# Reordered routed loop, a narrower block table, set 2's low parts on VectorE and no GpSimd drain at the end, in a gated-channel plus mixture-of-experts kernel

## The reference, cut to what matters

```python
def reference(x, cfc_w, bn_w, bn_b, router_w, w1, v1, w2, shared_gate, shared_up, shared_down):
    x = x + conv_gate(_ln_c(x))        # per channel gate from mean, max, std over pixels and a median
    t = _to_tokens(x)                  # 2048 tokens x 512 channels
    h = _ln_t(t)
    logits = h @ router_w.T            # 8 experts
    top_vals, top_idx = top_k(logits, 1)
    out = zeros_like(h)
    for e in range(8):                 # each token only counts for its expert
        out += dense_w[:, e:e+1] * ((silu(h @ w1[e]) * (h @ v1[e])) @ w2[e])
    out += (silu(h @ shared_gate.T) * (h @ shared_up.T)) @ shared_down.T
    return _from_tokens(t + out)
```

## Time and profile before

| what | value |
|---|---|
| median of 3 runs | 459.75 us (457.16 to 459.96) |
| the profiled execution's own time | 459.99 us |
| its span (first to last instruction) | 458.3 us |
| TensorE busy | 384.1 us, 84% of the span |
| VectorE, ScalarE, GpSimd busy | 264.0, 159.9 and 171.1 us |
| mean granted TensorE clock | 0.943 over the span, 1.00 from 250 to 440 us |
| TensorE busy from 300 to 350 us | 50.0 of 50 us |

### The profile page before, as it was taken

The page is one execution under the profiler, slowest core; times in us unless marked ns, Lnnn a source line. Parts: engine busy times, 40 slices in busy tenths (PEclk is TensorE's granted clock), DMA queues, the critical chain, the costliest instruction groups (busy, mean ns, idle before and its releaser), DMA issues.

```text
span 458.3 us, 7143 instructions
## 1 busy us (share of the span) xinstructions
PE 384.1 (84%) x1870; PEld 312.7 (68%) x1871; DVE 264.0 (58%) x496; ACT 159.9 (35%) x263; POOL 171.1 (37%) x213
## 2 busy tenths in 40 slices
PE   2444022999999999999979999999999999999980
PEld 2333011788888888888858777888887788777860
DVE  5985858446465656556596827627455745564320
ACT  4885841212323242222000344425153615352110
POOL 5772685002020212205822595532416242615110
PEclk9999555699999999999999999999999999999996
DMA  8800251101111111111331647855537772724110
GB/s 309 336 1 0 92 184 46 47 23 47 46 47 69 48 46 47 66 51 46 116 115 48 205 160 272 271 217 194 196 104 261 284 222 82 268 119 131 42 46 4
DMA packets 15867, 56.20 MB, mean 123 GB/s; under 512 B 2591, under 2 KB 2591, under 8 KB 12384
## 3 DMA queue, kind: packets, MB, share of 16 engines
q1 hardware_dynamic: 10960, 40.93, 24.8%
q0 software_dynamic: 4880, 14.95, 9.6%
HBM read 43.28 MB, written 13.63 MB: 124 GB/s over the span
## 4 chain that ended last, share of the span: by engine, by line
PE 77%; DVE 10%; issue 4%; POOL 3%; ACT 2%; DMA 1%; DVEq 0%; POOLq 0%
PE GU L1156 44%; PE yb L1156 22%; PE tx L1141 4%; PE th L1148 3%; PE th L1183 3%; DVE tiles L758 2%; DVE bn_parts L711 1%; DVE stats_rows L925 1%; PE mb L1134 1%; ACT tiles L538 1%; POOL tok_rstd L382 1%; DMA x_sb<-x_tok 1%; ACT scratch L549 1%; PE GU L1107 1%; DVE bn_parts L716 1%
## 5 line engine op out<-in xcount | busy, mean ns | idle before, releaser
L1156 PE MATMUL GU<-w_parts,xT 128*128 (+1 forms) x864 | 218.8, 403 | 3.2 <-issue 2.0
L1156 PEld LDWEIGHTS GU<-w_parts,xT 128*128 128x128 f32 x864 | 160.6, 191 | 38.9 <-issue 7.0
L1156 PE MATMUL yb<-w_parts,hT 128*128 (+1 forms) x432 | 109.2, 402 | 4.9 <-DVE hT L840 4.9
L1156 PEld LDWEIGHTS yb<-w_parts,hT 128*128 128x128 f32 x432 | 80.2, 191 | 22.9 <-issue 6.5
L613 ACT ACTIVATE hT<-th 128x512 fp32r<-128x512 f32 x36 | 21.6, 599 | 165.4 <-PE th L1148 165.4
L473 POOL DMA_INDIRECT out<-x_sb,scatidx x20 | 29.2, 1458 | 101.7 <-DVE x_sb L1037 101.4
L846 DVE TENSOR_TENSOR hidden<-hidden,GU 128x512 f32<-128x512 f32 x36 | 24.8, 688 | 61.8 <-issue 41.8
L603 ACT ACTIVATE xT<-tx 128x512 fp32r<-128x512 f32 x37 | 22.2, 599 | 90.6 <-PE tx L1141 90.6
L429 POOL TENSOR_TENSOR x_rstd<-x_mv,eps 128x1 f32<-128x1 f32 x16 | 3.5, 217 | 115.8 <-DVE x_mv L822 115.8
L1032 DVE TENSOR_TENSOR w_parts<-w_raw,w_parts 128x2048 f32 x19 | 43.5, 2289 | 5.3 <-ACT w_parts L526 3.0
L526 ACT ACTIVATE w_parts<-w_raw 128x2048 f32 (+1 forms) x24 | 45.1, 1909 | 0.3 <-issue 0.3
(11 more groups left out here) (205 smaller groups left out, 389.6 us busy)
## 6 DMA issues: line engine op xcount, KB each, us to landing
w_raw<-weights SPq DMA_DIRECT2D x27, 1024.0 KB, 5.1
x_sb<-x_tok SPq DMA_DIRECT2D x8, 512.0 KB, 6.9
xn_d<-tiles SPq DMA_DIRECT2D x16, 256.0 KB, 2.0
z_d<-x_sb SPq DMA_DIRECT2D x16, 256.0 KB, 2.1
tiles<-xn_d,tokidx POOLq DMA_INDIRECT x21, 4.0
x_sb<-z_d,tokidx POOLq DMA_INDIRECT x20, 5.4
out<-x_sb,scatidx POOLq DMA_INDIRECT x20, 4.0
conv<-conv_par SPq DMA_DIRECT2D x1, 10.0 KB, 9.5
```

Of the source, the lines that this page charges most:

```text
L1156: last = pe.matmul(dst, left[:, lp, kc, :], wset(q, k, wp, kc), start=(i == 0), stop=(i == 3 * KC - 1))
```

## The change

In the routed loop TensorE transposes x ahead of the up product; ScalarE's `x_hi` and VectorE's `x_lo` come ahead of `silu_gate` and `gated`, and both read the table behind these. The low part of UP is made behind `add_routed`. The table has 8 columns: TensorE reads one value for a set instead of two (slot and semaphore count are computed from it), VectorE three instead of seven, ScalarE four instead of seven, and only values with bounds are asserted. GATE and UP share one branch on ScalarE. At the entry VectorE makes the low parts of set 2's GATE and UP, which GpSimd made before. The block is opened with `no_gpsimd_drain=True`.

```diff
-SLOT_COL, READY_COL, SLOT2_COL, READY2_COL = range(4)
-TOTAL_COL = 4
-OTHER_COL, FIRST_COL, LOADED_COL, BEFORE_COL = range(8, 12)
-FLAG_COL, COLS = 12, 16
+SET_COL, SET2_COL, TOTAL_COL = range(3)
+DUE_GU_COL, DUE_DOWN_COL, AT_COL, FIRST_COL, COLS = range(4, 9)
...
-        block = ctx.enter_context(nc.Block())
+        block = ctx.enter_context(nc.Block(no_gpsimd_drain=True))
...
-            return [nc.s_assert_within(v, lowest.get(col, 0), highest.get(col, 1))
-                    for v, col in zip(got, cols)]
+            return [nc.s_assert_within(v, *bounds[col]) if col in bounds else v for v, col in zip(got, cols)]
...
             split_lo(1, DOWN)
-            split_lo(2, GATE)
             pool.wait_ge(z_out, 16 * NT)
             for b in range(RING - 1):
                 gather_z(b)
-            split_lo(2, UP)
...
-                for k in range(3):
-                    with act.If(due[k] > 0):
-                        act.wait_ge(w_in[k], loaded)
-
-                        act.wait_ge(y_done if k == DOWN else u_done, first + NT)
-                        split_hi(w_raw[:, k, :, :], w_parts[:, ds(other, 1), k, HI, :, :].rearrange("p a k c -> p (a k) c"))
+                for ks, due in (((GATE, UP), due_gu), ((DOWN,), due_down)):
+                    with act.If(due > 0):
+                        act.wait_ge(y_done if ks == (DOWN,) else u_done, first + NT)
+                        for k in ks:
+                            act.wait_ge(w_in[k], at * 16 + 32)
+                            split_hi(w_raw[:, k, :, :], w_parts[:, ds((at + 1) % 2, 1), k, HI, :, :].rearrange("p a k c -> p (a k) c"))
...
                 h_hi(b + NT, u % 2)
+                x_hi(b + (NT + 2), u % 2)
                 silu_gate(b + (NT + 1), 1 - u % 2)
-                entries = table_entries(act, b + 1, range(OTHER_COL, FLAG_COL + 3))
-                x_hi(b + (NT + 2), u % 2)
-                next_set(entries)
+                next_set(table_entries(act, b + 1, range(DUE_GU_COL, FIRST_COL + 1)))
...
+            def lo_of(k, at):
+
+                dve.wait_ge(whi, at * 3 + (k + 1))
+                dve.wait_ge(wlo, at * 3 + (k + 3))
...
+                dve.tensor_tensor(lo, w_raw[:, k, :, :], hi.bitcast(F32), ALU.subtract).then_inc(wlo, 1)
...
                 h_lo(b + NT, u % 2)
-                entries = table_entries(dve, b + 1, range(OTHER_COL, FLAG_COL + 3))
+                x_lo(b + (NT + 2), u % 2)
                 gated(b + (NT + 1), 1 - u % 2)
-                x_lo(b + (NT + 2), u % 2)
-                next_set(entries, (GATE, UP))
+                due_gu, due_down, at = table_entries(dve, b + 1, range(DUE_GU_COL, AT_COL + 1))
+                with dve.If(due_gu > 0):
+                    lo_of(GATE, at)
                 add_routed(b + NT, b, u, j * 16 + 16 * (base + 1))
-                next_set(entries, (DOWN,))
+                with dve.If(due_gu > 0):
+                    lo_of(UP, at)
+                with dve.If(due_down > 0):
+                    lo_of(DOWN, at)
...
             dve.wait_ge(tables, 1)
-            next_set(table_entries(dve, 0, range(OTHER_COL, FLAG_COL + 3)), (DOWN,))
+            lo_of(GATE, 1)
+            lo_of(UP, 1)
+            _, due_down, at = table_entries(dve, 0, range(DUE_GU_COL, AT_COL + 1))
...
-                q, ready, q_after, ready_after = table_entries(pe, b, range(SLOT_COL, READY2_COL + 1))
-                gate_product(n + 1, 1 - u % 2, 1 - u % 2, q_after, ready_after)
+                at, after = table_entries(pe, b, range(SET_COL, SET2_COL + 1))
+                gate_product(n + 1, 1 - u % 2, 1 - u % 2, after % 2, after * 3)
                 transpose_h(n, u % 2)
-                up_product(n + 1, 1 - u % 2, 1 - u % 2, q_after, ready_after)
 
                 pe.wait_ge(xg_in[ahead], j * 16 + 16 * (base + 1 + (u + 2) // RING))
                 transpose_x(n + 2, xg[:, ahead, :])
-                down_product(n, u % 2, q, ready)
+                up_product(n + 1, 1 - u % 2, 1 - u % 2, after % 2, after * 3)
+                down_product(n, u % 2, at % 2, at * 3)
```

51 lines of the change are left out of this document (20 added, 31 removed).

## The result

| | before | after |
|---|---|---|
| median | 458.47 us (457.16 to 459.96, 4 runs) | 448.1 us (446.9 to 450.0, 4 runs) |
| the profiled execution: own time, span | 459.99, 458.3 | 446.93, 445.1 |

The ratio is 0.9766 with a 95% interval of 0.9732 to 0.98: 2.3% faster.

The account below looks back on a forecast made before the run. TensorE, 77% of the 458.3 us span's chain, was taken as the bound. Terms -0.43 - 4.98 + 0.65 + 0.15 - 5.06 + 0.30 = -9.37 from 459.99, less 0.24 for the median, gave 450.4 us; range 448.8 to 455.6.

Parts of the forecast that it names:

- Start of the loop: First gate product of the loop: its 0.43 us wait for TensorE's sequencer goes whole with two assertions fewer.
- Order of a step: Routed loop: x transposed ahead of the up product and the table read last remove up to 4.98 us of TensorE gaps.
- Splits at the floor: Steps where GATE and UP are due: h_lo ends 1.2 us before the down product wants it, so they cost the floor.
- Entry: Loop entry: two splits of 2.29 us new on VectorE delay the first h_lo and down product, costing 0.65 us.
- End of the loop: Behind the last full step: one branch more on VectorE before the last h_lo, costing 0.15 us.
- The drain: End of the span: without GpSimd's DRAIN the barrier closes at once, saving the whole 5.06 us.
- the 0.30 for small waits: Six switch steps of the loop: unforeseeable small waits, estimated to cost 0.3 us, between 0 and 1.
- A: Loop entry: gathers of z are held by the splits moved to VectorE; time 451.2 us; chance 0.13.
- B: End of the kernel: the drain's 5.06 us only move to the barrier or behind the span; 455.5 us; chance 0.14.
- C: Switch steps: ScalarE's high parts come no earlier, h_lo stays late, some 0.5 us kept in each of six; 453.4 us; chance 0.06.
- D: Loop: TensorE waits for gathered x at the earlier transposes, 1.1 us in each of 18 steps; 470 us; chance 0.03.
- E: Loop gains nothing, its gaps only change names, and only the drain goes; 454.7 us; chance 0.04.

Follow-up runs that it names:

- the two drain runs: Kernel before with only the GpSimd drain left out: 454.7 us, ratio 0.9916; changed kernel with the drain put back: 451.97 us, ratio 0.9897.
- the run with the transposes put back: Changed kernel with transposes of x back behind the up product and x_hi, x_lo back behind silu and gated: 457.78 us, ratio 0.9985.
- the drain alone: Kernel before with only the GpSimd drain left out (no_gpsimd_drain=True): 454.7 us, ratio 0.9916.
- fewer assertions: Kernel before with assertions only on table values a step computes with (VectorE 2 in place of 7), order and columns unchanged: 458.74 us, ratio 0.9985.
- the second attempt: Changed kernel with set 1's UP and DOWN low parts made by VectorE instead of GpSimd, block_experts moved behind h_lo(n+3): 444.63 us, ratio 0.9687.

## Why the prediction was right or wrong

1. *Start of the loop, -0.43.* Right. The wait is gone; the stage got 0.28 us shorter besides, which I did not trace further.

2. *Order of a step, up to -4.98.* The sum was right, the reason was not. The prediction said that with the table read behind gated and x_lo "the seven assertions, 7 x 0.28 = 1.96 us, no longer stand in front of anything". They stand in front of the GATE split, and this is where they cost most: the order alone makes the kernel slower by 1.2%. Ahead of gated, where the trace showed 2.62 us, they cost at most 1 us. What saved the number, by luck as far as item 2 goes, is that item 3 worked with one assertion and not with seven. The forecast named the right gain for the two edits together and credited one of them.

3. *Splits at the floor.* Right: 1.28 us to spare against 1.2, and both signs at the switch steps (gap ahead of the split, gap ahead of the gate product) went as it said.

4. *Entry, +0.65.* 0.52 us, by the step's length (9.59 less 9.07), of which only 0.20 show as a gap. h_lo was forecast at 269.8 and started at 266.96, which is that moment less the 2.87 us (2.16 and 0.71) by which all of it had come forward. Two errors cancelled in it: the splits began 0.6 us later than forecast (262.15 and 2.87 are 265.02, against 264.4), and the reads of the table ran beside them (assertions from 265.6 on), so that h_lo followed the splits' end at 266.83 by 0.13 us and not by 0.56.

5. *End of the loop, +0.15.* 0.17.

6. *The drain, -5.06.* Right, shown from both sides (5.1 and 5.2 us).

The failed step is the floor: I held 9.13 us for what matmuls end to end give, and so called 4.98 "all that a better order can win". The order changed the floor too. By starts, a product that follows transposes is 2.81 to 2.85 us from the next start (283.47 to 286.28; in before 430.49 to 433.34), one that follows a product 2.72 (286.28 to 289.00). Before, up and down product both followed transposes; now the down product follows the up product, and the two sets of transposes stand together, which costs 0.08 us (264.00, 264.44, 264.79, against 0.35 and 0.36 in before). In sum that is 0.06 us in each of 18 steps and 0.08 in the last (6.41 to 6.33), 1.16 us. With 0.13 less at the entry and the 0.14 of the 0.30 for small waits that didn't come, it would make 1.43; the gaps of before were 4.85 us and not 4.98, since its last transposes follow at 6.41 us and not at 9.13 less 2.85. That leaves the loop's 1.3 us over the forecast.

The rest of the miss is the base. I took 459.75, the median of three runs (457.16, 459.75, 459.96); with a fourth at 457.18 it was 458.47. From its own base the change made -10.37 where -9.35 was forecast. The range's lower end let every cost fall to nothing, but held the one gain that it took for a ceiling.

The rivals. A happened and cost nothing. Timeline of GpSimd at the entry of after:

```profile
262.08 0.97 POOL L463 DMA_INDIRECT x_sb<-z_d,tokidx  x1 [5.69 <-DMA z_d<-x_sb]
263.36 1.90 POOL L463 DMA_INDIRECT x_sb<-z_d,tokidx  x1 [0.30 <-issue]
265.56 2.10 POOL L463 DMA_INDIRECT x_sb<-z_d,tokidx  x1 [0.30 <-issue]
```

Two of three gathers took twice as long beside VectorE's splits (262.15 to 266.83), but the first was issued 0.07 us before they began, and add_routed waited for TensorE alone.

I weighed a rule and an inference there (the Trainium skill, SBUF — State Buffer, section Who interferes with whom). Its rule that a VectorE operation with two inputs in SBUF contends with GpSimd's reads agrees with these rows, 1.90 and 2.10 us beside the splits against 0.97. Its inference that writing descriptors isn't held they can't decide: these gathers also read their row numbers (tokidx) from SBUF, so the delay may be the read's alone, and the prediction went too far in saying that the inference doesn't fit.

B is refuted by the two drain runs. C did not occur in the changed kernel; it is much like what the run with the transposes put back shows, where the split waits 2.38 us for ScalarE's high part. D did not occur: TensorE has no wait for a DMA in the loop. E is wrong by 5.3 us.

## What to carry to other kernels

A gap on an engine beside the critical one says where time stands, not what it costs: ask what would follow at once if it went, and what waits for that. Here 41.8 us of gaps were worth 1 us, and in the new order, behind gated, as many assertions cost 4.7. Where an edit reorders and another thins out what is reordered, predict the four corners, not the sum.

A floor read from the quietest step is the floor of that order of instructions alone.

## What the runs showed of the hardware

- The price of a wait on TensorE is more than the wait. Behind the gap of 2.95 us the next product took 4.18 and the next 3.37 us with a granted clock of 0.79 from 236 to 244 us: 1.7 us more than 3.00 and 2.88. Ten of the eleven traces with that gap show it (before has 4.58 and 2.89); in the one with the short table in the old order the gap is 2.93 us and the products took 3.00 and 2.88. So the same idle time sometimes lowers the clock and sometimes doesn't.
- A clock that has risen can fall back within 4 us. All 14 traces start the first product of token tiles at 80.5 to 80.7 us, behind a stretch in which TensorE was mostly idle. In nine it takes 3.97 to 4.59 us and the next one 3.0. In five (before, its repeat, the drain alone, fewer assertions, the second attempt) it takes 4.92 to 5.28 us; then the granted clock, at 1.00 by 86 us, is down to 0.50 by 89 to 90 us, behind two groups of eight 128x16 matmuls and 0.79 us of idle time (which the nine have too), and the next product takes 4.00 to 4.37 us. These five have their anchor at 225.3 to 225.7 us, the nine at 222.7 to 223.5. Why the first rise comes sooner or later stays open; nothing here tried it. And a record of the clock can miss a stretch: with the drain put back it reads 1.00 from 78 us on, though the first product took 3.97 us.
- A product of 12 matmuls that follows another product takes 0.1 us less by starts than one that follows transposes (2.72 against 2.81 to 2.85 us above).
- GpSimd's drain at the end of the block took 5.06 and 5.15 us with every scatter already waited for; those of the other engines took 7 to 17 ns.
